# A two-layer graph kernel: the transposes and the application of K stand one or two projections later in each step

## The reference

```
x = layernorm(x + einsum('bnf,nm->bmf', x, adj*adj) + bias)          # layer 0
z_l, z_g, v = h @ W_lang.T, h @ W_grav.T, h @ W_V.T                   # layer 1, h = x
A_l = relu(cosine similarity of the rows of z_l), zero diagonal
A_g = exp(-squared distance of the rows of z_g / (2 sigma^2)), zero diagonal
K   = w_l * rownormalise(A_l * adj) + (1 - w_l) * rownormalise(A_g * adj)
x = layernorm(h + (K @ v) @ W_O.T)
```

## Time and profile before

| | |
|---|---|
| times of three executions | 702.32, 702.46, 703.02 us |
| profiled execution: span from first to last instruction | 701.2 us |
| its own time | not listed apart; the median of the three stands 1.3 us above the span |
| TensorE busy (matmuls) | 671.6 us, 96% |
| VectorE busy | 536.3 us, 76% |
| ScalarE busy | 345.4 us, 49% |
| GpSimd busy | 211.0 us, 30% |
| granted TensorE clock, mean | 0.997 |
| DMA moved | 38.33 MB, 55 GB/s in the mean |

### The profile page before, as it was taken

One profiled execution on the slowest core, in us unless ns is written; L12 is line 12 of the kernel. 1 busy time (PEld: TensorE's weight loads), 2 busy tenths in 40 slices (PEclk: granted clock), 3 DMA queues, 4 the chain that ended last, 5 costly groups with the idle time before them and its releaser, 6 DMA issues. The chain is left out here.

```text
span 701.2 us, 11745 instructions
## 1 busy us (share of the span) xinstructions
PE 671.6 (96%) x3579; PEld 570.4 (81%) x3579; DVE 536.3 (76%) x1523; ACT 345.4 (49%) x614; POOL 211.0 (30%) x454
## 2 busy tenths in 40 slices
PE   8999999999999999999999999999999999999994
PEld 7888878787887878788787878878787887878883
DVE  6835795977879597786959778695977969697786
ACT  5633546355354535445453544545454454545433
POOL 0121413333341333334133333413333341233022
PEclk9999999999999999999999999999999999999998
DMA  7210020111102011110201111020111102001002
GB/s 286 91 38 24 5 86 31 61 60 61 61 3 87 30 60 60 60 60 0 90 30 60 60 60 60 0 90 30 60 60 60 55 5 90 31 0 61 0 31 91
DMA packets 20406, 38.33 MB, mean 55 GB/s; under 512 B 1824, under 2 KB 1824, under 8 KB 20384
## 3 DMA queue, kind: packets, MB, share of 16 engines
q1 hardware_dynamic: 20384, 38.05, 15.0%
HBM read 21.27 MB, written 16.78 MB: 54 GB/s over the span
## 5 line engine op out<-in xcount | busy, mean ns | idle before, releaser
L357 PE MATMUL ring<-hT_hi,T_hi 128*128 128x512 f32 x320 | 129.5, 405 | 0.0
L357 PE MATMUL ring<-hT_hi,T_lo 128*128 128x512 f32 x320 | 125.2, 391 | 0.0
L357 PE MATMUL ring<-hT_lo,T_hi 128*128 128x512 f32 x320 | 125.0, 391 | 0.0
L562 ACT ACTIVATE yT_hi<-ring 128x512 fp32r<-128x512 f32 x128 | 75.7, 591 | 71.0 <-PE ring L357 70.4
L774 DVE TENSOR_TENSOR yT_lo<-ring,yT_hi 128x512 fp32r<-128x512 f32 x128 | 86.1, 682 | 26.7 <-ACT yT_hi L562 26.7
L357 PE MATMUL ring<-M_hi,hT_hi 128*128 128x512 f32 x256 | 101.5, 397 | 0.0
L357 PE MATMUL ring<-M_hi,hT_lo 128*128 128x512 f32 x256 | 100.2, 391 | 0.0
L357 PE MATMUL ring<-M_lo,hT_hi 128*128 128x512 f32 x256 | 99.8, 390 | 0.0
L1074 POOL TENSOR_TENSOR x_lo<-x_sb,x_hi 128x512 fp32r<-128x512 f32 x60 | 77.0, 1315 | 18.5 <-ACT x_hi L562 18.5
L614 ACT ACTIVATE o_sb<-o_sb,z_nb,z_rs 128x512 f32<-128x512 f32 x60 | 47.1, 809 | 63.9 <-POOL z_nb L1086 63.9
L784 DVE CUSTOM_DVE_ANT_0 diag_scr<-P_sb,ident 128x128 f32<-128x128 f32 x128 | 29.7, 288 | 62.9 <-ACT P_sb L562 62.9
(11 more groups left out here) (159 smaller groups left out, 1421.9 us busy)
## 6 DMA issues: line engine op xcount, KB each, us to landing
x_sb<-in_x_dram SPq DMA_DIRECT2D x15, 1024.0 KB, 5.2
out_dram<-o_sb SPq DMA_DIRECT2D x60, 256.0 KB, 2.0
x_sb<-in_x_dram SPq DMA_DIRECT2D x2, 512.0 KB, 5.2
w_raw<-in_L_gnn_W_lang_dram SPq DMA_DIRECT2D x1, 1024.0 KB, 6.2
o_sb<-in_L_gnn_W_grav_dram SPq DMA_DIRECT2D x1, 1024.0 KB, 8.6
h_sb<-in_L_gnn_W_V_dram SPq DMA_DIRECT2D x1, 1024.0 KB, 10.7
w_raw<-in_L_gnn_W_O_dram SPq DMA_DIRECT2D x1, 1024.0 KB, 7.8
out_dram<-x_sb SPq DMA_DIRECT2D x4, 256.0 KB, 2.0
```

Of the source, the lines that this page charges most:

```text
L357: last = pe.matmul(bank[:, :], a, b, start=n == 0, stop=n == len(terms) - 1)
L562: return act.activation(dst, src, ACT.Copy, scale=scale)
```

## The change

In `step`, on each of the three engines, the transposes of K and what hangs on them stand later. On TensorE `transpose_k(0)` comes behind projection 5 instead of behind projection 4, `apply_k(0)` and `apply_k(1)` come behind projection 7 instead of behind 6, and `transpose_k(1)` comes behind the two applications. ScalarE evicts in the matching order. On VectorE `lo_proj(4)` and `lo_proj(5)` go ahead of `lo_kt(0)` and `combine(1)`, `lo_proj(7)` goes ahead of `add_z(0)`, and `lo_kt(1)` goes between `add_z(0)` and `count_z(0)`.

```diff
 TensorE, step
                 project(g, par, 4)
+                project(g, par, 5)
                 if tail:
                     transpose_k(g - 1, 0)
-                project(g, par, 5)
                 project(g, par, 6)
+                project(g, par, 7)
                 if tail:
                     apply_k(g - 1, 0)
                     apply_k(g - 1, 1)
-                project(g, par, 7)
-                if tail:
                     transpose_k(g - 1, 1)
                 layer0(g + 1, 0)
 ScalarE, step
                 hi_proj(g, 4)
                 if tail:
-                    hi_kt(g - 1, 0)
                     scale_l(g - 1, 1)
                 hi_proj(g, 5)
+                if tail:
+                    hi_kt(g - 1, 0)
                 hi_proj(g, 6)
                 hi_proj(g, 7)
                 if tail:
                     hi_kt(g - 1, 1)
+                hi_proj(g, 8)
+                if tail:
                     normalise_out(g - 1, 0)
                     normalise_out(g - 1, 1)
-                hi_proj(g, 8)
 VectorE, step
                     similarities(g - 1, 1)
                     coefficients(g - 1, 1)
+                lo_proj(g, 4)
+                lo_proj(g, 5)
+                if tail:
                     lo_kt(g - 1, 0)
-                lo_proj(g, 4)
-                if tail:
                     combine(g - 1, 1)
-                lo_proj(g, 5)
                 lo_proj(g, 6)
+                lo_proj(g, 7)
                 if tail:
                     add_z(g - 1, 1 - par, 0)
+                    lo_kt(g - 1, 1)
                     count_z(g - 1, 0)
-                lo_proj(g, 7)
-                if tail:
-                    lo_kt(g - 1, 1)
                 add_y(g + 1, 1 - par, 0)
```

## The result

The changed kernel takes 704.08 us (median of 20 executions, 703.70 to 705.96), the kernel before 702.60 us beside it (20 executions). The ratio is 1.0021, with a 95% interval of 1.0015 to 1.0028. It is slower by 1.5 us, and since the whole interval lies above 1, this small loss is not noise. The forecast was 703.2 us in a range of 701.0 to 705.0.

What follows compares the result with a forecast made beforehand. TensorE, busy 96% of the span, bounds the kernel, so its holes set the time. 14 x (-0.69 moved into the hole + 0.74 given back) = +0.7 us on the median 702.46 gives 703.2 us, range 701.0 to 705.0.

Steps and rivals of the forecast that it cites:

- The first transposes keep their place against VectorE: TensorE ahead of K's first transposes: projection 5 fills 0.69 us of the hole without moving them; alone 9.7 us gained.
- Projection 7 waits for `lo_proj(4)`: Projection 7 needs projection 4's ring bank, so TensorE waits and starts at 2.62; 0.3 us of the wait is open.
- K's low part decides: VectorE idles for projection 5's copy, so `lo_kt(0)` ends at 4.24, after projection 7 has issued at 4.11; the application waits.
- The application and the second transposes: TensorE: application at 4.30 after a 0.06 hand-over, second transposes at 5.78 against 5.73, 0.05 us later per step.
- rival B: Dearer hand-over: the application takes over from VectorE in 0.15 instead of 0.06, +2.0 us, 704.4 us; chance 0.22.
- The first distance behind the transposes: TensorE: the first matmul distance after a hole is longer, 0.32 instead of 0.23 us.
- Nothing behind is late: Behind the second transposes: VectorE reaches `add_y` about 0.75 us later, but slack of 1.8 us makes this cost nothing.
- The sum: Over 14 steps, 0.69 moved into the hole and 0.74 given back at two new waits: +0.7 us, 703.2 us.
- The chances: Against a border of about 0.2%, 1.4 us: faster 0.13, same 0.61, slower 0.26.
- Rival A: The hole is really filled: K's eviction does not bind but projection 7 does, -3.5 us, 699.0 us; chance 0.13.
- Rival C: VectorE's lag of 0.75 us comes through behind the second transposes: +10.5, 713 us; chance 0.03.
- Rival D: TensorE's clock falls to 1.2 GHz because of three shorter holes per step: +80, 783 us; chance 0.01.

Runs made afterwards that it cites:

- run 1: The changed kernel with `hi_kt(0)` back ahead of the scaling and `lo_kt(0)` directly behind `lo_proj(4)`: 699.88 us.
- run 3: The kernel before with only the eviction orders of ScalarE and VectorE changed, TensorE's order kept: 723.86 us.
- run 7: The changed kernel with one wait, on K's low part, ahead of each application instead of two, except in the last group: 703.67 us.
- run 8: The changed kernel with two or five further VectorE instructions, results unused, ahead of `count_z(0)`: 704.09 us with two, 722.06 us with five.
- run 4: The kernel before with only the first transposes of K moved behind projection 5: 696.02 us.
- run 6: The changed kernel with the two waits ahead of each application swapped, so that K's low part is waited for last: 704.45 us.

## Why the prediction was right, and where it was off

- *The first transposes keep their place against VectorE.* Right. L806 ends 0.15 ahead of them in both kernels, and the hole shrank by 0.68 (predicted 0.69).
- *Projection 7 waits for `lo_proj(4)`.* Right: it starts at 2.65 (predicted 2.62), 0.32 later than the pace would have it (predicted 0.3).
- *K's low part decides.* Right: it ends at 4.22 (4.24), ScalarE's copy of projection 5 starts at 2.60 (2.60), VectorE idles 0.71 for it (338.31 to 339.02, predicted 0.74). Runs 1 and 3 show that this is the term that decides, not only that it is there.
- *The application and the second transposes.* In the odd steps the application is at 4.28 (4.30) and the second transposes at 5.78 (5.78). In the six even steps of the loop they are at 5.84, so here the size was off. The step that was mis-sized is the hand-over: I took 0.06 for all steps, and it was 0.14 in six of them. The row behind the 0.06 was the first matmul of a projection, which has one wait ahead of it; the application has two. That is rival B's size, in part of the steps, but not for its reason: run 7 shows that it goes with the waits, not with the kind of instruction. It adds 6 x 0.07 = 0.4 us to the 0.7.
- *The first distance behind the transposes.* Its value of 0.32 is right, its reason (a hole ahead) is not, as shown above. The sum does not change.
- *Nothing behind is late.* Right: `add_y` is at 8.94 against 8.18, and no TensorE wait came there. Run 8 shows how much more would have been needed.
- *The sum.* Predicted +0.7, measured +1.5. In the profiles, the way from the first of all these transposes to the last grew by 1.14 (88.93 to 687.91 against 89.35 to 687.19). That is the 0.7 and the 0.4. The other 0.3 us I can't place. In the profiles of all kernels here the first of these transposes start between 88.9 and 89.8 us, though no kernel changes what they wait for; so this much may lie in the start-up, which is not shown.
- *The chances.* The prediction drew its border at 0.2%, 1.4 us. The measured 1.5 us lies just beyond it, on the side that had 0.26; "same" had 0.61. The measured 704.08 us is also nearer to rival B's 704.4 than to the forecast's 703.2. The traces decide between them: eight steps took the forecast's hand-over and six took B's. Rival A was near at hand: one eviction further ahead (run 1) and its 699 us would have come. Rival C is refuted by run 8. Rival D did not come: the mean granted clock of whole executions was 0.993 to 0.997 in both kernels, and it was 1.00 in a whole step of the changed kernel, from hole to hole (the columns are the stretch, its us, the busy us of PE, PEld, DVE, ACT and POOL, the granted clock, the DMA's share and GB/s):

```profile
293.75:334.87 41.12, 40.37 (x214) 33.59 (x212) 32.43 (x93) 20.46 (x36) 13.35 (x28) 1.00 0.14 53
```

What the prediction did not say is that the two halves of the change work against each other. It had both numbers, 0.69 moved into the hole and 0.74 given back, but not that the first is to be had without the second (run 4), since in the old order the applications hide the ring wait.

## What to carry to other kernels

When work is moved into a hole ahead of a wait, ask of each moved piece what it was hiding at its old place: here projection 5 hid next to nothing (in run 4 the application starts 0.05 to 0.14 behind K's low part), but the applications hid an eviction for projection 7, and moving projection 7 gave back more than projection 5 brought. Fill the hole with work that depends on nothing of the current chain (layer 0 of the next group), and keep the eviction that the next matmul waits for ahead of any instruction that itself waits. In a kernel that is bound by one engine in order, such a schedule can be followed, from starts and hand-overs, to within 0.1 us per step (5.78 forecast, 5.77 to 5.86 measured).

## What the runs showed of the hardware

TensorE's hand-over from a VectorE eviction to a matmul depends on the waits ahead of the instruction. With one wait it was 0.06 us in all steps at the application (run 7), and 0.05 to 0.06 at projection 7 of the changed kernel. With two and the late one last, it was 0.14 to 0.15 (run 6, `KT_lo` to application); the first transposes of K, which also have two waits with the late one last, start 0.14 to 0.15 behind the addition in the changed kernel and in the one before. That fits, but no run separates it from what a transpose itself may cost. With two and the late one first, it was 0.06 in the odd steps and in step 14, which stands behind the loop, and 0.14 in the loop's even steps. Why the loop's two halves differ was not found out.

A 128x512 matmul that starts behind a hole also has a longer distance to the next one, 0.33 to 0.34 us instead of 0.23 (0.30 to 0.31 in run 6), so such a hole costs about 0.1 us beside its own length. Ahead of the transposes a hole does not: from the transposes to the second matmul behind them it is 0.48 with the hole (335.81 to 336.29) and 0.45 without (341.59 to 342.04).
